# The first block's copy of the projected rows in DRAM, laid out by operand half, parity, row and unit

## The reference

```python
# first block: B=16, D=128 (channels), T=256 (positions), NH=8, dk=16
q = transpose(x) @ Wq.T                       # (B, T, D)
qh = q.reshape(B, T, NH, dk).transpose(0, 2, 1, 3)
scores = scale * einsum('bhqd,bhkd->bhqk', qh, qh)
logits = (scores * cmask + (1 - cmask) * NEG) * rmask
ctx = einsum('bhqk,bhkd->bhqd', softmax(logits), qh)
x = x + transpose(ctx @ Wo.T)
# second block: adaptive layer norm from cond, 16-head attention, gelu feed-forward, both residual
```

## Time and profile before

| | |
|---|---|
| median of three runs | 788.14 us |
| profiled execution | 792.2 us, span 790.0 us, mean granted clock 0.974 |
| TensorE busy over the span | 756.6 us (96%) |
| first block, to the first matmul of L790 in the chain | 0 to 197.84 us |
| scores of groups 1 to 7 begin at | 38.95, 60.96, 79.78, 98.59, 117.40, 136.21, 154.51 us |
| DMA share in the first block, 20 us to 150 us | 0.72 to 1.09 in stretches of 10 us |

### The profile page before, as it was taken

How to read it: one execution, slowest core, us unless ns; L and a number is a source line. 1 busy time by engine, 2 the same in 40 slices (tenths; PEclk the granted TensorE clock), 3 DMA queues, 4 the chain that set the end, 5 groups by cost and what they waited for, 6 DMA issues and landing times.

```text
span 790.0 us, 12978 instructions
## 1 busy us (share of the span) xinstructions
PE 756.6 (96%) x4763; PEld 621.5 (79%) x4763; DVE 394.5 (50%) x801; ACT 439.5 (56%) x1194; POOL 142.5 (18%) x133
## 2 busy tenths in 40 slices
PE   7799999986999999999999999999999999899997
PEld 4455555555888888888988888988898888778886
DVE  5656666664235534444545443555544435446444
ACT  2557767671465554455655447465454485557653
POOL 4134443100232111111111111111111223200000
PEclk9979999995899999999999999999999999999999
DMA  3989888701332221221212212212222232221001
GB/s 114 180 214 208 214 193 190 143 27 47 126 121 94 68 81 67 68 81 54 80 64 72 80 66 66 71 62 80 81 68 69 69 117 94 67 80 40 30 12 53
DMA packets 67707, 73.30 MB, mean 93 GB/s; under 512 B 3936, under 2 KB 47960, under 8 KB 67656
## 3 DMA queue, kind: packets, MB, share of 16 engines
q1 hardware_dynamic: 67192, 72.40, 32.6%
q10 hardware_dynamic: 464, 0.22, 0.1%
HBM read 46.36 MB, written 26.25 MB: 92 GB/s over the span
## 4 chain that ended last, share of the span: by engine, by line
PE 70%; DVE 3%; ACT 2%; DMA 1%; issue 0%; DVEq 0%; SPq 0%; ACTq 0%
PE bank L790 27%; PE pair L790 14%; PE ring L790 13%; PE ring L1076 7%; PE pair L1062 7%; PE ring L116 1%; DVE x1l L1304 1%; ACT x1h L1164 1%; PE ring L1095 0%; ACT probs L1183 0%; DMA x1f<-in_L_cond_ffn_w_dram 0%; PE ring L1031 0%; DVE ol L1337 0%; DVE pB L1315 0%; DMA turned<-pB 0%
## 5 line engine op out<-in xcount | busy, mean ns | idle before, releaser
L1183 ACT ACTIVATE probs<-pair,nm 128x128 f32<-128x128 f32 x256 | 98.2, 485 | 183.7 <-DVE nm L1326 183.7
L1439 POOL TENSOR_TENSOR probs<-probs,rinv 128x512 f32<-128x512 f32 x64 | 66.6, 1041 | 357.0 <-DVE rinv L1334 357.0
L790 PE MATMUL bank<-x1h,w_hi 128*128 128x512 f32 x256 | 112.1, 438 | 5.6 <-DVE x1l L1304 5.5
L678 DVE TENSOR_REDUCE mx<-ring 128x2 fp32r<-128x512 f32 x128 | 79.8, 683 | 45.1 <-PE ring L446 45.1
L790 PE MATMUL bank<-x1l,w_hi 128*128 128x512 f32 x256 | 101.5, 396 | 0.0
L790 PE MATMUL bank<-x1h,w_lo 128*128 128x512 f32 x256 | 101.3, 396 | 0.0
L611 ACT ACTIVATE pt<-ring 128x512 f32<-128x512 f32 x128 | 70.3, 595 | 45.0 <-PE ring L458 45.0
L1357 DVE COPY Vv<-pair 128x512 f32<-128x512 f32 x64 | 44.2, 691 | 81.0 <-PE pair L790 81.0
L790 PE MATMUL pair<-w_hi,x1l 128*128 128x256 f32 x256 | 72.8, 284 | 0.0
L790 PE MATMUL pair<-w_lo,x1h 128*128 128x256 f32 x256 | 72.6, 283 | 0.0
L790 PE MATMUL pair<-w_hi,x1h 128*128 128x256 f32 x256 | 72.3, 282 | 0.0
(11 more groups left out here) (206 smaller groups left out, 1518.4 us busy)
## 6 DMA issues: line engine op xcount, KB each, us to landing
turned<-pB SPq DMA_DIRECT2D x63, 256.0 KB, 2.0
pT<-turned SPq DMA_DIRECT2D x63, 256.0 KB, 2.7
stage<-in_L_cond_qkv_w_dram SPq DMA_DIRECT2D x12, 512.0 KB, 9.5
QS<-qd SPq DMA_DIRECT2D x14, 384.0 KB
qd<-qh SPq DMA_DIRECT2D x14, 256.0 KB
KS<-qd SPq DMA_DIRECT2D x14, 256.0 KB
mb<-in_cond_dram SPq DMA_DIRECT2D x8, 256.0 KB, 9.6
kept<-X SPq DMA_DIRECT2D x1, 2048.0 KB, 8.0
```

What stands on the lines that cost most here:

```text
L678: dve.tensor_reduce(mx[:, 2 * b + s, :], ring[:, 2 * b + s, :].rearrange("p (k q) -> p k q", k=2), AX_X, ALU.max, negate=True).then_inc(dv ...
L790: last = nc.tensor.matmul(bank, w(k), x(k), start=(start and i == 0), stop=(stop and i == len(terms) - 1))
L1183: last = nc.scalar.activation(plain(probs)[:, t] if direct else probs[:, :, b, :].rearrange("p c a -> p a c"), Sb[:, t] if direct else Sb[ ...
L1439: pool.tensor_tensor(w, w, r, ALU.mult).then_inc(pool_p, 1)
```

## The change

`qd` was (group parity, head, part, row, 512): for a given partition of an operand the four units' rows of 512 lie 192 KB apart. It becomes (group parity, part, head parity s, row, unit j, 512): the four units' rows lie next to each other, one piece of 2048 elements or 8 KB. `gather` writes its rows of 2 KB into the new places, `spread` reads pieces of 8 KB. Parts, sizes, semaphores and the order of issue are the same.

```diff
-        qd = nc.dram_tensor("qd", (2, NH, 3, DK, 512), F32).ap()
+        qd = nc.dram_tensor("qd", (2, 3, 2, DK, 4, 512), F32).ap()
...
                     for c in (0, 2):
-                        sp.dma_start(q[:, c], qh[:, :].bitcast(F32)).then_inc(l_qd[g % 2], 16)
+                        sp.dma_start(q[c].rearrange("s d j n -> j (s d) n"),
+                                     qh[:, :].bitcast(F32)).then_inc(l_qd[g % 2], 16)
                     sp.wait_ge(dve_ql, g)
-                    sp.dma_start(q[:, 1], ql[:, :].bitcast(F32)).then_inc(l_qd[g % 2], 16)
+                    sp.dma_start(q[1].rearrange("s d j n -> j (s d) n"), ql[:, :].bitcast(F32)).then_inc(l_qd[g % 2], 16)
...
-                    v = qd[g % 2].rearrange("(j s) c d n -> s (c d) j n", s=2)
+                    v = qd[g % 2].rearrange("c s d j n -> s c d (j n)")
                     sp.wait_ge(l_qd[g % 2], LG * nth(g))
                     for s in range(2):
                         for dst, r, c, n in ((KS, 0, 1, 2), (KS, 2, 0, 1), (QS, 0, 0, 3)):
                             r = 64 * s + r * DK
-                            sp.dma_start(dst[r:r + n * DK, g % 2, :, :].bitcast(F32),
-                                         v[s, DK * c:DK * (c + n)]).then_inc(l_q[g % 2], 16)
+                            sp.dma_start(dst[r:r + n * DK, g % 2, :, :].bitcast(F32).rearrange("p j n -> p (j n)"),
+                                         v[s, c:c + n]).then_inc(l_q[g % 2], 16)
```

## The result

The changed kernel takes 902.95 us (median of 6 runs, 901.62 to 906.67), the kernel before 788.93 us in the same comparison (6 runs, 786.65 to 792.05). The ratio is 1.1436 with a 95% interval of 1.1404 to 1.1469. The profiled execution took 901.83 us with a span of 899.7 us, against 792.2 and 790.0 before.

What follows compares the result with a forecast made beforehand. TensorE is busy 96%; the serial spread-gather loop has 0 to 3 us slack. 7 x (4.1 + 10.8) = 104.3, less 3.0, plus 3.2 makes 104.5; 788.1 + 104.5 = 892.6, say 892 us, range 870 to 930.

Steps and rivals of the forecast that it cites:

- The engines: DMA engines follow the outermost DRAM dimension: gather writes on 4, spread reads on 2, 3 or 16; gather share 0.25.
- First gather: Each gather puts 96 pieces on each of 4 engines, 8.2 us in place of 4.1: 4.1 us added.
- The cycle: Spread and gather in series, each group: 19.1 + 14.9 = 34 us, from 4.1 us more gather and 10.8 more spread.
- slack of 3.0 us: Before the change, group 7's spread lands at 151.5 us and its scores start at 154.51; 3.0 us taken off the loss.
- Group 7: Its start moves later by seven gathers and spreads in series, 7 x (4.1 + 10.8) = 104.3 us, less 3.0 slack.
- Behind it: After group 7's start: 3.2 us more for TensorE at 1.2 GHz after idling, everything later as before.
- SyncE's waits for `qd`: Sign in SyncE's queue: these waits grow from 15.2 us to about 7 x 9 or more.
- The range's low end: 870 us: half taken of the 36 us that a spread of 16.1 us would save, which gives 856.
- C: Rival, faster: engines stay as many, spread takes 3.9 us in place of 10.5, group 1's wait goes: 781 us; chance 0.06.
- D: Rival, no change: transfers are cut as before and nothing moves, 788 us; chance 0.04.
- B: Rival: only the gather narrows, the spread is cut as before; cycle 23.2 us, 814 us; chance 0.05.
- A: Rival: narrow spread reads also collide, halving the rate of one long part, 5.2 us a group, 929 us; chance 0.10.

Runs made afterwards that it cites:

- twelve-read kernel: The changed kernel with each spread read cut by part into reads of 16 rows, twelve in place of six, gather as changed: 827.49 us, ratio 1.0467.
- kernel with near pieces: The kernel before with the copy laid out (part, row, head, column), 2 KB pieces 4 KB apart in place of 192 KB: 789.42 us, ratio 1.0005.
- fast kernel with two writes: The kernel before with the first spread's parity 1 reads on ScalarE's queue and the high part written to DRAM once, not twice: 794.59 us, ratio 1.0051.
- slow kernel with the wide gather: The changed kernel with each gather write cut by unit into four of 32 rows, 16 engines each, spread as changed: 875.93 us, ratio 1.110.

## Why the prediction was right, step by step

**The engines: right.** Shares of 0.26 for the 4-wide gather, 0.19 and 0.12 for the middle and the end of the 3- and 2-wide reads, and a changed kernel that is as fast as before once the outermost dimensions are wide (792.36). The Trainium skill's rule for the number of engines (DMA: Bandwidth & Descriptors, "Why a DMA increments its semaphore by 16 and not by 1") agrees with each of these. My share of 0.25 for the gather in the changed kernel itself was wrong, 0.14: two of its four engines finish beside the spread.

**First gather:** 4.1 us later predicted, first spread issued at 28.84 in place of 24.94, 3.9 measured.

**The cycle:** 34.0 predicted, 35.4 measured. Its terms were mis-sized. The spread took 25.6 us from issue to the group's start, predicted 12 + 10.8 = 22.8. One part of the 2.8 us is the price of the 16-row reads: the two of them put an 8 KB piece on every engine at once, which costs 1.0 us a piece by the twelve-read kernel, 1.4 us more than 2 x 0.32. The other part is mostly landing. The 12 us of before were 1.3 to the first data and 10.5 of data, which leaves 0.2 for landing. In the changed kernel the last 8 KB pieces move until about 127.2 us and the group starts at 128.53, 1.3 us later. The wide spreads that TensorE waited for say the same: 14.0 us from issue to start at group 1 of the kernel before (24.94 to 38.95), 12.9 at group 5 of the kernel with near pieces (103.60 to 116.52), not 12. So the slack of 3.0 us was too large as well, nearer 1 to 2. The step behind the spread gave 1.4 us back: it takes 9.5 us in most groups and 9.8 in the mean, where 34.0 - 22.8 = 11.2 was implied.

**Group 7:** predicted at 151.5 + 104.3 = 255.8 us, measured 267.49: 6 x 1.4 from the cycles and 3.3 from the last spread. The 259 us that the prediction names as a sign has in it the 3.2 us that its own sum puts behind the start of group 7.

**Behind it: mis-sized.** I added 3.2 us for the slow clock of group 7; its four units take 2.2 us more to the last one's start. Yet from the start of group 7 to the end of the span the changed kernel takes 899.7 - 267.49 = 632.2 us, the one before 790.0 - 154.51 = 635.5. The rest is 5.5 us shorter, 3.7 in the tail of the first block and 1.9 in the second block, and the change is not what made it so. The second block takes 590.3 us here and 592.2 before, but 590.4 in the fast kernel with two writes (from 203.65 to 794.0 us). In the tail, from the last unit's start to the first matmul of the second block, TensorE's granted clock differs between the two profiled executions: the changed kernel (284.39 to 309.39 us), and below it the kernel before (169.18 to 197.84):

```profile
284.00:309.00 25.00, 18.05 (x137) 13.20 (x129) 13.43 (x42) 8.38 (x16) 0.00 (x0) 0.90 0.11 37
```

```profile
169.00:198.00 29.00, 21.66 (x134) 16.02 (x131) 13.45 (x42) 8.16 (x16) 0.00 (x0) 0.69 0.12 39
```

0.90 against 0.69 of full speed, 25.0 us against 28.7. But the kernel with near pieces, as fast as the one before, has the short tail (25.0 us), and the slow kernel with the wide gather the long one (29.2 us), in this order:

```profile
169.00:194.00 25.00, 18.11 (x137) 13.17 (x129) 13.42 (x42) 8.43 (x16) 0.00 (x0) 0.91 0.11 36
```

```profile
254.00:284.00 30.00, 22.53 (x138) 16.76 (x131) 13.53 (x42) 8.04 (x15) 0.00 (x0) 0.67 0.12 40
```

So the tail's clock does not go with the change; why it falls in some executions earlier than in others is open. The profiled sum closes: 101.3 predicted up to the start of group 7, 11.7 missed there, 3.3 less behind it, 109.7; measured 901.83 - 792.2 = 109.6. With the 2.2 us alone behind it the sum is 115.2. By medians the change costs 114.0 us; the profiled execution of before was 3.3 us above its median, that of after 1.1 us below. The prediction of 104.5 was thus some 10 us low, by a spread whose landing and 16-row reads were priced too low.

**Signs that missed.** SyncE's waits for `qd` came to 42.5 us, not to 7 x 9 or more. SyncE spent the time elsewhere: it was held while it issued the gather's writes (12.19 and 6.47 us at group 3), and came to the wait later. The range's low end was worked out loosely: half of the 36 us under 892 is 874, not 870.

**The rivals.** C (faster) falls twice: the engines do fall, and 8 KB pieces on 16 engines move at 161 GB/s as 2 KB pieces did. D falls with it. B is the twelve-read kernel, 827 for 814. A falls too: two engines at the end of a spread move 25.5 GB/s each, an 8 KB piece still takes 0.32 us, and what is left of the spread's time after landing and the 16-row reads is 0.3 us, not the 5.2 of A. Pieces were slower only where sixteen engines wrote at once.

## What to carry to other kernels

Before rearranging a DRAM tensor for longer contiguous pieces, read what its new order does to the outermost dimension of every DMA on both sides: here 48 became 3, 32 became 2 and 8 became 4, and 8 KB pieces on two or three engines lost to 2 KB pieces on sixteen by 14%. A small DMA share beside a long wait for a DMA is the sign. And where all engines are busy at a low rate, ask first how many partitions they write, before the length or the distance of the pieces.

## What the runs showed that was not expected

- SyncE itself was held: the issue of two gather writes behind a narrow spread took 12.19 us in place of 1.26, and one chunk of weights 16.75 us. An issuing engine seems to be stopped once one DMA engine has much queued; here the transfers were late anyway.
- An 8 KB piece costs 0.32 us when two or three engines write and about 1.0 us when 16 engines write 16 partitions together.
- Two queues fill the two halves of the partitions at 202 GB/s in place of 151, without a gain in time. That other loads, which then run beside the one that is waited for, take the gain is a guess: with the 1 MB load moved away there was none either.
